# Later projections of a four-layer image kernel on 64x64 tiles of TensorE, with the images of odd pairs exchanged

## What is computed

```
L0: q, k = relu(x wq), relu(x wk) (8 wide); v = x wv
    y = softmax(q k^T) v + x                         # 256 x 256 weights per image
L1: h = group_norm(y, 32 groups)
    z = softmax((h Wq)(h Wk)^T / 8) (h Wv) Wo + y
L2: q, k, v = z in_proj; 8 heads of width 8; each token looks at 7 neighbours of a hexagon
    s = layernorm(z + attention(q, k, v) out_w)
    u = layernorm(s + relu(s w1) w2)
L3: relu(u + conv1x1(relu(conv3x3_grouped(relu(conv1x1(u))))))   # with batch norms folded in
```

## Time and profile before

| | |
|---|---|
| median of 3 runs | 111.4 us (111.35 to 111.5) |
| the profiled execution's own time | 110.48 us |
| its span, first to last instruction | 108.4 us |
| busy: PE, DVE, ACT, POOL | 98.2, 70.2, 52.4, 32.1 us |
| granted TensorE clock over the span | 1.00 |
| bytes moved by DMA | 2.88 MB |

### The profile page before, as it was taken

How to read it: one execution, slowest core, us unless ns; L and a number is a source line. 1 busy time by engine, 2 the same in 40 slices (tenths; PEclk the granted TensorE clock), 3 DMA queues, 4 the chain that set the end, 5 groups by cost and what they waited for, 6 DMA issues and landing times.

```text
span 108.4 us, 2128 instructions
## 1 busy us (share of the span) xinstructions
PE 98.2 (91%) x794; PEld 56.1 (52%) x794; DVE 70.2 (65%) x166; ACT 52.4 (48%) x139; POOL 32.1 (30%) x46
## 2 busy tenths in 40 slices
PE   4978699799999999899998999998999998999960
PEld 1435468586758676566553735565322222467420
DVE  2029957989999968897999997692652522200292
ACT  2317936796969698974161400241647454200220
POOL 8960000739190980000010377782000201100000
PEclk9999999999999999999999999999999999999999
DMA  2990000000000000000000000000000000000005
GB/s 81 307 396 39 0 0 0 6 0 6 0 0 0 6 0 0 0 0 0 0 6 0 0 0 0 0 0 0 0 0 6 0 0 0 6 0 6 0 3 193
DMA packets 1593, 2.88 MB, mean 27 GB/s; under 512 B 176, under 2 KB 1200, under 8 KB 1584
## 3 DMA queue, kind: packets, MB, share of 16 engines
q1 hardware_dynamic: 1152, 2.09, 5.4%
q10 hardware_dynamic: 432, 0.67, 1.9%
HBM read 2.23 MB, written 0.52 MB: 25 GB/s over the span
## 4 chain that ended last, share of the span: by engine, by line
PE 64%; DVE 17%; ACT 6%; POOL 4%; issue 4%; DMA 3%; DVEq 0%
PE bank L873 7%; PE bank L893 7%; PE quad L862 6%; PE quad L1142 5%; PE bank L1072 4%; DVE ffh L261 4%; PE quad L1111 4%; PE bank L1122 3%; ACT prob L440 3%; PE quad L1052 3%; PE duo L1098 3%; DMA p<-in_p 3%; PE duo L1142 3%; PE duo L942 2%; DVE ffh L734 2%
## 5 line engine op out<-in xcount | busy, mean ns | idle before, releaser
L440 ACT ACTIVATE prob<-quad,nmax 128x256 f32<-128x256 f32 x32 | 14.8, 477 | 2.1 <-DVE nmax L621 2.1
L447 ACT ACTIVATE probT<-bank 128x512 f32<-128x512 f32 x16 | 9.6, 602 | 6.1 <-PE bank L873 6.1
L621 DVE TENSOR_REDUCE nmax<-quad 128x2 f32<-128x512 f32 x16 | 10.7, 678 | 2.4 <-PE quad L862 2.4
L873 PE MATMUL bank<-pv,probn 128*128 128x128 f32 x64 | 10.1, 280 | 1.8 <-DVE probn L630 1.1
L630 DVE TENSOR_SCALAR probn<-prob,rrec 128x256 f32<-128x256 f32 x32 | 10.5, 371 | 0.6
L873 PEld LDWEIGHTS bank<-pv,probn 128*128 128x128 f32 x64 | 7.2, 141 | 5.1 <-DVE probn L630 4.1
L544 ACT ACTIVATE sq<-bank,prep2t 128x512 f32<-128x512 f32 x4 | 2.7, 687 | 14.3 <-PE bank L1072 10.9
L862 PE MATMUL quad<-k,q 32*128 32x256 f32 (+1 forms) x64 | 8.1, 400 | 1.5 <-DVE k L612 0.7
L1142 PE MATMUL quad<-pads,ctaps 32*32 32x512 f32 x144 | 9.2, 595 | 0.0
L1142 PE MATMUL bank<-pads,ctaps 32*32 32x512 f32 x72 | 9.2, 596 | 0.0
L1142 PE MATMUL duo<-pads,ctaps 32*32 32x512 f32 x72 | 8.8, 593 | 0.0
(11 more groups left out here) (176 smaller groups left out, 209.9 us busy)
## 6 DMA issues: line engine op xcount, KB each, us to landing
p<-in_p SPq DMA_DIRECT2D x1, 1012.5 KB, 6.9
xT<-in_xT SPq DMA_DIRECT2D x4, 128.0 KB, 3.8
p<-in_p ACTq DMA_DIRECT2D x1, 448.0 KB, 5.0
out_dram<-xT SPq DMA_DIRECT2D x1, 256.0 KB, 2.1
out_dram<-xT SPq DMA_DIRECT2D x2, 128.0 KB, 1.7
pv<-in_pv ACTq DMA_DIRECT2D x1, 128.0 KB, 3.2
p<-in_p ACTq DMA_DIRECT2D x1, 74.5 KB, 3.0
```

Source lines behind the costliest of these rows:

```text
L440: s.activation(prob[:, n % 3, b, :], S_BANK[n % 4][:, b * TOK:(b + 1) * TOK], ACT.Exp, bias=nmax[:, n, b:b + 1], accum_out=rsum[:, n, b:b ...
L447: s.activation(flat(probT[:, n % 4, :, :]), T_BANK, ACT.Copy).then_inc(probT_sb, 1)
L621: v.tensor_reduce(nmax[:, n, :], S_BANK[n % 4].rearrange("p (b m) -> p b m", b=BLK), AX.X, ALU.max, negate=True).then_inc(max_ready, 1)
L873: ins = nc.tensor.transpose(T_BANK[:, mb * TOK + b * 128:mb * TOK + b * 128 + 128], probn[:, n % 2, b, mb * 128:mb * 128 + 128], ident)
```

## The change

All projections from L1 on become products on 64x64 tiles of the array, one per image, instead of 128x128 products with a half-empty matrix. A tile is set by the partitions it reads (the image's half) and the partitions it writes; four such tiles exist, and two kinds of output are made at once so that all four are in use. The output of some lands in the other image's half. So the images of pairs 1 and 3 are exchanged in the input on the host, and centring and out projection put them back. In particular:

- L1: queries stay in their half, keys come out exchanged. ACT evicts the keys in two instructions of 64 partitions that exchange the halves back. Both queries and keys are now signalled together, at the end of four products.
- L2: queries and values of a pair are four products, keys two more. Queries and keys come out exchanged, and the head sums read their table rolled by 64 rows. The value projection moves ahead of the second transposes, into a bank that the scores used.
- Centring and out projection take an even and an odd pair together: four products of N = 256. The odd pair goes to the other half. The two images' halves lie in two banks (`D_IN`).
- PSUM banks are given out anew, and the order on PE behind `cast(1)` is another.

```diff
+        D_IN = [psum[:, 4:6, 0:TOK], psum[:, 0:2, 0:TOK]]
+        D_OUT = [bank[4], bank[1]]
+        FF_BANKS = [(bank[2], bank[3]), (bank[5], bank[7])]
-        CONV2_BANKS = [bank[7], bank[4], bank[0], bank[1]]
+        CONV2_BANKS = [bank[4], bank[0], bank[2], bank[1]]
+        HALF = (slice(0, 64), slice(64, 128))
-        PROJ2 = [(bank[6], bank[7], bank[6])] * 2 + [(bank[2], bank[0], bank[1]), (bank[3], bank[4], bank[5])]
+        PROJ2 = [(bank[6], bank[7], bank[0]), (bank[6], bank[7], bank[1]),
+                 (bank[2], bank[0], bank[1]), (bank[3], bank[4], bank[5])]
...
             def keys_queries1(j):          # ACT
-                act.wait_ge(qkv1_ps, 3 * j + 1)
+                act.wait_ge(qkv1_ps, 3 * j + 2)
                 s.activation(q1[:, j, :], W_BANK[0][:, 0:TOK], ACT.Identity, bias=qb[:, :], ...)
-                act.wait_ge(qkv1_ps, 3 * j + 2)
-                s.activation(k1[:, j, :], W_BANK[1][:, 0:TOK], ACT.Identity, bias=kb[:, :])\
+                s.activation(k1[HALF[0], j, :], W_BANK[1][HALF[1], 0:TOK], ACT.Identity, bias=kb[HALF[1], :])
+                s.activation(k1[HALF[1], j, :], W_BANK[1][HALF[0], 0:TOK], ACT.Identity, bias=kb[HALF[0], :])\
                     .then_inc(k1_sb, 1)
...
             def project1(j):               # PE
+                for i in range(2):
+                    mm(W_BANK[0][HALF[i], 0:TOK], wqk1g[HALF[i], 64 * i:64 * i + 64], hT[HALF[i], j, :], ...)
+                    ins = mm(W_BANK[1][HALF[1 - i], 0:TOK], wqk1g[HALF[i], 128 + 64 * i:192 + 64 * i], hT[HALF[i], j, :], ...)
+                ins.then_inc(qkv1_ps, 2)
+            def project2_queries_values(j):
+                for i in range(2):
+                    mm(PROJ2[j][0][HALF[1 - i], 0:TOK], inT[HALF[i], 0, 64 * i:64 * i + 64], zT[HALF[i], j, :], ...)
+                    ins = mm(PROJ2[j][2][HALF[i], 0:TOK], inT[HALF[i], 2, 64 * i:64 * i + 64], zT[HALF[i], j, :], ...)
+            def project2_keys(j):
+                for i in range(2):
+                    ins = mm(PROJ2[j][1][HALF[1 - i], 0:TOK], inT[HALF[i], 1, 64 * i:64 * i + 64], zT[HALF[i], j, :], ...)
...
                 if u >= STEADY:
-                    project2(u - STEADY, 0)
-                    project2(u - STEADY, 1)
+                    project2_queries_values(u - STEADY)
+                    project2_keys(u - STEADY)
                 transposes(2 * u + 1)
-                    project2(u - STEADY, 2)
...
             def centre_input(gr):
+                if gr == 0:                # waits for keys and values of pair 3
+                else:
+                    pe.wait_ge(avprod_sb, QUARTERS * (PAIRS - 1) + 2)
+                for i in range(2):
+                    own = HALF[i]
+                    mm(D_IN[gr][own, 0, :], centre[own, own], zT[own, 2 * gr, :], start=True, stop=False)
+                    mm(D_IN[gr][HALF[1 - i], 1, :], centre[own, own], zT[own, 2 * gr + 1, :], start=True, stop=False)
+            def out_single(gr):            # the odd pair's seventh product: two tiles
+            def out_sums(gr):
+                j = 2 * gr
+                pe.wait_ge(avsum_sb, 2 * j + 4)
+                for k in range(NB // 2):
+                    for i in range(2):
+                        own = HALF[i]
+                        mm(D_IN[gr][own, 0, :], outc[own, own], value_sums[j][own, k, :], ...)
+                        ins = mm(D_IN[gr][HALF[1 - i], 1, :], outc[own, own], value_sums[j + 1][own, k, :], ...)
...
             cast(0)
             centre_input(0)
             exp_sums(1)
             cast(1)
-            centre_input(1)
-            out_sums(0)
             cast(2)
-            out_single(1)
-            out_sums(1)
+            out_single(0)
+            out_sums(0)
             cast(3)
             variance(0)
-            out_sums(2)
-            out_single(3)
-            out_sums(3)
+            centre_input(1)
+            out_single(1)
+            out_sums(1)
...
-    part["head_sum"][:, 16:32] = np.kron(np.eye(16), np.ones((HD, 1)))
+    part["head_sum"][:, 16:32] = np.roll(np.kron(np.eye(16), np.ones((HD, 1))), 64, axis=0)
+    x = f["x"].reshape(PAIRS, 2, TOK, CH).copy()
+    x[1::2] = x[1::2, ::-1]
```

More of the change, by code:

```diff
@@ L75, in sem @@
             return ctx.enter_context(nc.semaphore(name))
[L78 to L81, removed]
+        psum = ctx.enter_context(nc.psum_tensor("psum", [128, 8, 512], F32))
+        bank = [psum[:, i, :] for i in range(8)]
         S_BANK = bank[0:4]
@@ L328, in image_rows, with ln_input, halves_like @@
             return ap.rearrange("p (j a b) -> p j a b", j=2, b=SIDE)
+        def ln_input(n):
+            return D_IN[n] if n < GROUPS else D_OUT[n - GROUPS]
+        def halves_like(ap, n):
+            return ap.rearrange("p (a b) -> p a b", b=TOK) if n < GROUPS else ap
         def halves_of(c, h):
@@ L559, in relu_ff @@
                 act.wait_ge(ff_ps, FH * gr + h + 1)
-                s.activation(hidden[gr][:, h, 0, :], bank[h], ACT.Relu, bias=b1f[:, h:h + 1]).then_inc(ff_act, 1)
+                s.activation(hidden[gr][:, h, 0, :], FF_BANKS[h][0], ACT.Relu, bias=b1f[:, h:h + 1]).then_inc(ff_act, 1)
             def conv1_out(gr):
@@ L568, in conv1_out @@
                 c = 2 * gr
-                s.activation(middle(c), image_rows(bank[c]), ACT.Relu, bias=bnsh1[:, :]).then_inc(c1_act, 1)
+                s.activation(middle(c), image_rows(CONV1_BANKS[gr][0]), ACT.Relu, bias=bnsh1[:, :]).then_inc(c1_act, 1)
             def conv2_out(gr):
@@ L777, in conv1_out @@
                 c = 2 * gr + 1
-                v.tensor_scalar(middle(c), image_rows(bank[c]), bnsh1[:, :], 0.0, ALU.add, ALU.max)\
+                v.tensor_scalar(middle(c), image_rows(CONV1_BANKS[gr][1]), bnsh1[:, :], 0.0, ALU.add, ALU.max)\
                     .then_inc(c1_dve, 1)
@@ L1025, in _ @@
             attend(ROUNDS - 1)
-            project2(2, 0)
-            project2(2, 1)
-            project2(3, 0)
-            project2(3, 1)
+            project2_queries_values(2)
+            project2_keys(2)
+            project2_queries_values(3)
+            project2_keys(3)
             head_sums(0)
@@ L1032, in _ @@
             prepare2()
-            project2(2, 2)
-            project2(3, 2)
             head_sums(2)
@@ L1055, in centre_input @@
             def centre_input(gr):
-                pe.wait_ge((k2_sb, v2_sb)[gr], PAIRS)
-                mm(D_BANK[gr], centre, zT[:, 2 * gr:2 * gr + 2, :].rearrange("p a b -> p (a b)"),
-                   start=True, stop=False)
-            def out_single(j):
-                o = D_BANK[j // 2][:, TOK * (j % 2):TOK * (j % 2) + TOK]
-                pe.wait_ge(avprod_sb, QUARTERS * j + QUARTERS)
-                mm(o, outc, products[j][:, NB - 1, :], start=False, stop=False)
-            def out_sums(j):
-                o = D_BANK[j // 2][:, TOK * (j % 2):TOK * (j % 2) + TOK]
-                pe.wait_ge(avsum_sb, 2 * j + 2)
-                for k in range(NB // 2):
-                    ins = mm(o, outc, value_sums[j][:, k, :], start=False,
-                             stop=j % 2 == 1 and k == NB // 2 - 1)
+                if gr == 0:
+                    pe.wait_ge(k2_sb, PAIRS)
+                    pe.wait_ge(v2_sb, PAIRS)
+                else:
[5 more added lines that the diff above has]
+            def out_single(gr):
+                j = 2 * gr + 1
+                pe.wait_ge(avprod_sb, QUARTERS * j + QUARTERS)
+                for i in range(2):
+                    own = HALF[i]
+                    mm(D_IN[gr][HALF[1 - i], 1, :], outc[own, own], products[j][own, NB - 1, :], start=False, stop=False)
+            def out_sums(gr):
+                j = 2 * gr
+                pe.wait_ge(avsum_sb, 2 * j + 4)
+                for k in range(NB // 2):
+                    last = k == NB // 2 - 1
+                    for i in range(2):
+                        own = HALF[i]
+                        mm(D_IN[gr][own, 0, :], outc[own, own], value_sums[j][own, k, :], start=False, stop=last)
+                        ins = mm(D_IN[gr][HALF[1 - i], 1, :], outc[own, own], value_sums[j + 1][own, k, :],
+                                 start=False, stop=last)
                 ins.then_inc(av_used, 1)
@@ L1110, in feed_forward1 @@
                     own = slice(64 * i, 64 * i + 64)
-                    ins = mm(bank[FH * i + h], w1g[own, 128 * h:128 * h + 128], xhat[own, gr, :],
+                    ins = mm(FF_BANKS[h][i], w1g[own, 128 * h:128 * h + 128], xhat[own, gr, :],
                              start=True, stop=True)
@@ L1115, in feed_forward2 @@
             def feed_forward2(gr):
-                mm(D_BANK[gr], centre_g[:, :], xhat[:, gr, :], start=True, stop=False)
+                mm(D_OUT[gr], centre_g[:, :], xhat[:, gr, :], start=True, stop=False)
                 for h in range(FH):
@@ L1134, in conv1 @@
                     own = slice(64 * i, 64 * i + 64)
```

(2 more changed lines are left out.)

89 lines of the change are left out of this document (47 added, 42 removed).

## The result

The changed kernel takes 114.16 us (median of 4 runs, 112.65 to 115.44) against 111.45 for the kernel before (4 runs, 111.35 to 111.66): a ratio of 1.021, interval 1.012 to 1.030. Forecast were 111.59, in a range of 110.4 to 112.5. It is slower, and by more than the range allowed.

A forecast was written before the change was run, and what follows sets the result against it. It took PE and DVE to bound rounds 2 to 4, ACT's loop rounds 6 and 7, then DVE, and PE alone behind 75.45. Terms +0.14 + 0.20 - 0.15 = +0.19 on 111.4 gave 111.59, range 110.4 to 112.5.

The forecast's parts named there:

- Prices: PE unit prices: four 64x64 tiles at once 0.43, change of tile shape about 0.15, transposes behind it 0.59.
- Rival A: Every four-tile step: row halves sharing a PSUM bank take turns, 0.86 a step, 117.8 in all; chance 0.03.
- rival B: Four-tile steps on the path: weight loads show between passes, 0.05 a pass, 112.9 or half, 112.2; chance 0.24.
- Rival D: Whole kernel: each us of PE saved is a us of time, some 6 us, 105.4; chance 0.03.
- Rounds 2 to 4, 0: project1 of pairs 0 to 2: PE arrives 0.33 earlier but must wait for DVE's statistics; gain 0.
- Rival C: Rounds 2 to 5 pay, through earlier DVE statistics or half evictions at 0.24: 110.4 to 111.0; chance 0.25.
- Round 5, +0.14: project1 of pair 3: scores wait for the second half of the keys' eviction and start 0.14 later.
- Rounds 6 and 7, +0.20: project2 of pairs 0 and 1: transposes end 0.10 later in each round, moving ACT's weight copy; cost +0.20.
- Last `attend` to cast(0), 0: Products for pairs 2 and 3 shrink, but DVE is the bound there; gain 0.
- Weighted sums and out projection, -0.15: cast(3) starts earlier, gaining 0.10, and `out_sums(1)` gives 0.05 more: 0.15 gained at the first feed-forward product.
- Behind, 0: From the feed-forward on: same operations on other banks, 0, with +-0.05 each for two squarings and two normalisations.
- a fall of the clock at +1.5: Ahead of cast(2) PE idles 2 us; should its clock fall, later work takes twice as long for a while, +1.5.

The follow-up runs named there:

- the gap filled: Changed kernel plus two products of zeros (128x128, N = 512) between cast(1) and cast(2), in PE's idle time: 112.02 us, ratio 1.009.
- both kernels that separate them: Changed kernel with two products of zeros and the old project1: 111.31 us; kernel before with only the new projections of L1 and L2: 112.24 us.
- four kernels with two products of zeros: Zeros ahead of cast(2) in: changed kernel, 112.02; that with old project1, 111.31; kernel before with new centring and out projection, 111.15; that with cast(3) split, 111.59.
- the gap filled and `project1` as it was: Changed kernel with two products of zeros, L1's queries and keys from two 128x128 products, keys evicted whole: 111.31 us, ratio 1.000.
- the new out projection alone: Kernel before with new centring, out projection, their order and banks, and two products of zeros ahead of cast(2): 111.15 us, ratio 1.000.
- reordered one: Kernel before, all old 128x128 products, with cast(2) moved directly behind cast(1): 115.11 us, ratio 1.038.

## Why the prediction was wrong

Step by step, against what the trace with the gap filled shows, so at the full clock the sum assumed:

- Prices. Four 64x64 tiles 0.43, change of shape 0.15, transposes behind them 0.59: right, measured 0.60 to the transposes. Rival A is refuted (it wanted 0.86 a step), rival B as far as weight loads go (0.05 a pass): passes follow each other 0.21 apart in `out_sums`, and the eight loads of a step start within 0.1 us. Rival D is refuted with them: PE spends what it saves in waits. On rival A's ground, that rows sharing a bank take turns, the Trainium skill ("TensorEngine Tiling (Array Packing)", Restrictions and Gotchas) and this measurement differ where the tiles write different partitions; here the measurement decides.
- Rounds 2 to 4, 0: right, and for the reason given. The load of the group statistics is released by DVE. Rival C's first half is refuted by it.
- Round 5, +0.14: measured +0.39. The mechanism was right, the scores wait for the second half of the keys; the size was off. Taken back by the 1.06 us of the start, the queries start at 38.42 and not at 38.38 (0.04), the two intervals are 0.50 and 0.49 and not 0.43 (0.13), and the scores start 0.14 behind the end of the keys and not 0.05 (0.09). Rival C's cheap half evictions, 0.24, are refuted: 0.47 each.
- Rounds 6 and 7, +0.20: measured 0.21 to 0.22, in both kernels that separate them.
- Last `attend` to cast(0), 0: measured 0.02 to 0.04.
- Weighted sums and out projection, -0.15: measured -0.07 alone, -0.1 in the changed kernel with the gap filled (+0.62 at cast(0), +0.53 at the feed-forward).
- Behind, 0: measured -0.01.
- At full clock the sum should have been +0.53 (0.39 + 0.22 + 0.02 - 0.1) instead of +0.19. That alone puts the kernel at 111.9, still in the range.

The step that failed is the one that was not in the sum. The sum was made at the granted clock of before, 1.00, throughout. Paragraph D of the rivals saw that "PE will idle 2 us ahead of cast(2)" and priced a fall of the clock at +1.5, near the 1.66 of the shorter one, but said that it "belongs with B", a rival about weight loads, and gave it no chance and no term of its own. Measured: a lower mean clock in all 10 runs of the changed kernel, in the two traces a fall for 3.4 and for 6.8 us, worth 1.66 and 3.31. Of the 3.84 us lost behind the start in the first profile the clock made 3.31, and of the 2.7 between the medians some 0.53 remain for the tiles and the order, by the trace at full clock.

The trace of before had the sign of it. The stretch from cast(1) to cast(2) was full (PE busy 3.58 of 3.66 us; the earlier trace rows show the out projection's loads at 64.56 and cast(2) at 66.06), because the order put the centring and the first sums into DVE's time. The forecast worked out rightly that this work was not on the path, and went on as if work off the path had no other use. It had: it kept the clock up. The gain that this order was to bring, DVE's 0.70 at cast(2), was indeed won, and lost again at cast(3) as forecast, where DVE waits 1.54 with the gap filled (1.6 forecast); so the move earned 0.1 and put 3.3 at stake.

What stays open: what decides between 3.4 and 6.8 us; why a gap of 1.1 us is followed by a fall in nine runs and not in three; and whether the falls in spite of the filling are more than chance. They are 3, 0, 0 and 2 of 12 in the four kernels with two products of zeros, where the kernel before itself has 5 of 52, and none of them has a trace. Whether the start of a run, early or late, has a part in it is open too.

No version beat the kernel before. The two that tie with it (the gap filled and `project1` as it was; the new out projection alone) have intervals of +-0.5% about 1.

## What to carry to other kernels

Before work is moved out of an idle stretch of PE, ask what the stretch looks like without it: work that is on no critical path may still be what holds the clock at 2.4 GHz, and in this kernel 2 us of idle PE were followed by up to 6.8 us at 1.2 GHz, which cost up to 3.3 us. In this kernel a smaller matmul paid only where PE was what came last; where PE already arrived on time beside another engine, its saving turned into a wait of about the same length, and the extra instruction that it handed to ACT was paid for as soon as ACT was what came last (round 5, 0.39).

## What the runs showed of the hardware

- The clock did not fall in the idle time but after it: 1.1, 1.3, 1.8 and 1.2 us after PE had work again (four traces, idle 2.08, about 2.1, 1.95 and 1.07). So the products that pay begin a microsecond or more behind the gap.
- With an idle time of about 2 us the clock fell in 16 of 16 runs (changed kernel 10, reordered one 6), with 1.1 us in 9 of 12, with 0.2 us in 5 of 48 (four kernels), which is no more than in the kernel before, where PE is busy 3.58 of 3.66 us at this place (5 of 52). The Trainium skill ("TensorE: Matmul & The Clock Gate", Part 1) says that the gate follows how busy PE has been of late; the runs agree, with these counts.
- The first record of 2.4 GHz stands at 6.0 to 6.5 us or at 10.2 to 11.0 us from the start, differently in two executions of one kernel; the later one has `scores(2)` 1.04 us later (13.10 against 12.06 in the changed kernel), five times the forecast's sum.
- ACT's evictions of 64 and of 128 partitions took the same 0.47 us for 256 columns; with the key eviction split in two they started 0.49 to 0.50 apart, whole ones 0.43.
- Two banks filled by four 64x64 tiles, both row halves in each, took the time of one 128x128 product, 0.43 us, with starts 0.02 us apart.
